# A delta-rule attention and feed-forward kernel: half of the triangular blocks inverted by GpSimd during the projection, key norms taken by token, key products stored unmasked, ScalarE copying only the blocks below the diagonal

## What is computed

```
q, k, v = silu(causal conv of 4 taps(x @ W.T));  beta = sigmoid(x @ Wb.T)
q, k = q/|q|, k/|k|                                  # norms by head and token
# per head, in chunks:  M = I + tril(beta*k @ k.T, -1);  T = M^-1
# u = T @ (beta*v);  w = T @ (beta*k)
# scan:  u_adj = u - w @ S;  o = q @ S + tril(q @ k.T) @ u_adj;  S += k.T @ u_adj
o = p0*fir3(v) + p1*fir15(v) + p2*fir63(v) + p3*o + p4*v     # p: softmax gates
x = layernorm(x + rmsnorm(o) @ Wo.T)
x = layernorm(x + ffn(x))                                    # 256-1024-1024-1024-256
```

## Time and profile before

| | us |
|---|---|
| median of three runs (2434.59 to 2437.62) | 2437.59 |
| the profiled execution | 2435.2 |
| its span in the trace | 2433.3 |
| projection, weights and FIR, recurrence: start | 0, 360.45, 612.28 |
| feed-forward: start | 1098.46 |
| TensorE, VectorE, ScalarE, GpSimd busy | 2157.0, 1235.5, 895.2, 593.4 |

### The profile page before, as it was taken

How to read it: one execution, slowest core, us unless ns; L and a number is a source line. 1 busy time by engine, 2 the same in 40 slices (tenths; PEclk the granted TensorE clock), 3 DMA queues, 4 the chain that set the end, 5 groups by cost and what they waited for, 6 DMA issues and landing times.

```text
span 2433.3 us, 40589 instructions
## 1 busy us (share of the span) xinstructions
PE 2157.0 (89%) x15412; PEld 1855.9 (76%) x15412; DVE 1235.5 (51%) x1872; ACT 895.2 (37%) x1425; POOL 593.4 (24%) x416
## 2 busy tenths in 40 slices
PE   7887865655699999967999999999999999999998
PEld 6776754555588888855888888888888888888887
DVE  5776758896477777762323332333333333323332
ACT  4554530002233334313434443444344334433442
POOL 2555555896344444430000000000000000000000
PEclk9999987887799999987999999999999999999999
DMA  3558759787989989925000000000000000000000
GB/s 131 194 197 204 194 200 211 198 207 236 241 229 249 250 235 241 254 79 219 1 18 17 0 17 17 17 0 17 17 17 0 17 17 17 0 17 17 18 1 18
DMA packets 346603, 257.53 MB, mean 106 GB/s; under 512 B 281394, under 2 KB 315698, under 8 KB 336434
## 3 DMA queue, kind: packets, MB, share of 16 engines
q1 hardware_dynamic: 333682, 232.65, 35.1%
q10 hardware_dynamic: 12864, 24.12, 2.8%
HBM read 156.85 MB, written 99.88 MB: 106 GB/s over the span
## 4 chain that ended last, share of the span: by engine, by line
PE 52%; issue 1%; DVE 1%; ACT 0%; DMA 0%; SPq 0%; POOL 0%; DVEq 0%; ACTq 0%; POOLq 0%
PE B L1611 46%; PE O L1639 5%; PE T L1567 1%; DVE yb L1738 0%; ACT gate L1677 0%; DMA wr<-wr_s 0%; SPq L1500 0%; DVE stats L1769 0%; ACT L1677 0%; DVE z L1764 0%; DVE z L1760 0%; DVE z L1783 0%; POOL rstd L1819 0%; SPq L1514 0%; DVEq L1733 0%
## 5 line engine op out<-in xcount | busy, mean ns | idle before, releaser
L1611 PE MATMUL B<-act1l,wr 128*128 128x512 f32 x1024 | 398.4, 389 | 0.0
L1611 PE MATMUL B<-act1h,wr 128*128 128x512 f32 x1024 | 398.3, 389 | 0.0
L1611 PE MATMUL B<-act0h,wr 128*128 128x512 f32 x1024 | 398.3, 389 | 0.0
L1611 PE MATMUL B<-act0l,wr 128*128 128x512 f32 x1024 | 398.3, 389 | 0.0
L1691 ACT ACTIVATE yb<-B,scol 128x512 f32<-128x512 f32 x256 | 176.2, 688 | 581.0 <-PE B L1611 581.0
L1726 DVE TENSOR_TENSOR act0l<-yb,act0h 128x512 fp32r<-128x512 f32 x256 | 176.1, 688 | 377.9 <-ACT act0h L1694 375.7
L1816 POOL TENSOR_TENSOR rstd<-mv,ln_eps 128x4 f32<-128x4 f32 x16 | 3.2, 199 | 1309.2 <-DVE mv L1777 1309.2
L379 DVE SCALAR_TENSOR_TENSOR acc<-proj,taps,acc 128x512 f32<-128x512 f32 x288 | 214.4, 750 | 92.3 <-ACT acc L334 83.7
L1726 DVE TENSOR_TENSOR act1l<-yb,act1h 128x512 fp32r<-128x512 f32 x128 | 88.6, 692 | 295.5 <-ACT act1h L1694 295.5
L224 PE MATMUL proj<-xt,w_qkv 128*128 128x262 f32 x768 | 195.0, 400 | 35.9 <-DMA xt<-in_xt 19.4
L1611 PEld LDWEIGHTS B<-act1h,wr 128*128 128x128 f32 x1024 | 192.2, 188 | 39.9
(11 more groups left out here) (164 smaller groups left out, 3477.6 us busy)
## 6 DMA issues: line engine op xcount, KB each, us to landing
qk_s<-yT SPq DMA_DIRECT2D x16, 1024.0 KB, 5.8
kk_s<-kfull SPq DMA_DIRECT2D x16, 1024.0 KB, 3.9
qk<-qk_s SPq DMA_DIRECT2D x16, 1024.0 KB, 6.7
lt<-kk_s SPq DMA_DIRECT2D x15, 1024.0 KB, 5.3
wraw<-in_ffn_w ACTq DMA_DIRECT2D x16, 704.0 KB, 6.4
wr_s<-wround ACTq DMA_DIRECT2D x16, 704.0 KB, 9.5
toe<-in_firp SPq DMA_DIRECT2D x64, 160.0 KB, 3.6
xt<-in_xt SPq DMA_DIRECT2D x16, 524.0 KB, 4.0
```

What stands on the lines that cost most here:

```text
L1611: last = nc.tensor.matmul(B[slot % 4][:, :], w, part, start=(k == 0 and i == 0), stop=(k == kts - 1 and i == len(parts) - 1))
```

## The change

- **Projection.** GpSimd no longer picks diagonals or masks. It squares the keys by token (`sqk`, from `ktok`), and VectorE reduces that, 128x1024 in place of 128x512, into `kk`. `kfull` is stored once, unmasked, as soon as it is copied; `a_s` is gone; after each step four DMAs bring its blocks from `kk_s` into `tri`.
- After step 8 VectorE computes the block scales of the first 8 steps (`first_scales`, after one Exp on ScalarE); TensorE turns them and ScalarE copies them out in step 10. GpSimd then runs the substitution of those blocks (4 of 8 slots), in steps 10 to 15 and after the last, columns 1 to 24.
- **Weights and FIR.** GpSimd zeroes the other half's upper parts, runs columns 25 to 30 and the row scaling of its half, then enters the loop. VectorE does the other half, both operations of a column in each of the first 30 groups. `toe` is laid out in full on the host and comes as one DMA of 768 KB for each 8 channels. `d_s` and `t_s` are stored by halves after the loop's SyncE iterations 2, 4, 18 and 20.
- **Recurrence.** VectorE zeroes `nmat` once; ScalarE copies N in three pieces of a bank (only what lies below the diagonal blocks); and the copies of round A stand ahead of the wait for `mixed`.

```diff
+EARLY_COLS = {10: (1, 5), 11: (5, 9), 12: (9, 12), 13: (12, 15), 14: (15, 18), 15: (18, 21), 16: (21, 25)}
+EARLY_END = 25
-def blocks_in(queue, io, keep, part):
+def blocks_in(queue, io, keep, t):
+    first = t * NS % P
     for q in range(NQ):
+        queue.dma_start(keep["tri"][first:first + NS, q * NSUB + t // EARLY_STEPS, :, :],
+                        io["kk_s"][q * CH:q * CH + CH, t * NS:t * NS + NS, q * CH:q * CH + CH].rearrange("i n j -> n i j")
+                        ).then_inc(keep["tri_in"][t // EARLY_STEPS], 16)
+class Substitution:
+    def outer_product(self, j):
+        row = self.tri[:, :, j, 0:j]
+        row = bass.AP(tensor=row.tensor, offset=row.offset, ap=[row.ap[0], row.ap[1], [0, CH - 1 - j], row.ap[2]])
+        return self.engine.tensor_tensor(self.products(j), bcast(self.tri[:, :, j + 1:CH, j], j), row, ALU.mult)
+    def update(self, j):
+        below = self.tri[:, :, j + 1:CH, 0:j]
+        return self.engine.tensor_tensor(below, below, self.products(j), ALU.add)
...
@@ project: SyncE
                     sp.wait_ge(kk_out, 4 * n)
-                    for q in range(NQ):
-                        sp.dma_start(io["a_s"][rows, bass.ds(t * NS, NS), :], kfull[p][rows, :, rows]).then_inc(diag_stored[p], 16)
+                    sp.dma_start(io["kk_s"][:, t * NS:t * NS + NS, :], kfull[p][:, :, :]).then_inc(kk_stored[p], 16)
...
-                    sp.wait_ge(kk_masked, n)
-                    sp.dma_start(io["kk_s"][:, bass.ds(t * NS, NS), :], kfull[p][:, :, :]).then_inc(kk_stored[p], 16)
+                    sp.wait_ge(kk_stored[p], 16 * (t // 2 + 2))
+                    blocks_in(sp, io, keep, t)
@@ project: VectorE, values_out
-                    dve.wait_ge(diag_picked, t * NQ + NQ)
...
-                    nc.vector.tensor_reduce(kk[...], picked[p][:, :, :], AX.X, ALU.add).then_inc(kk_summed, 1)
+                    dve.wait_ge(sqk_done, t + 3)
+                    nc.vector.tensor_reduce(kk[...], sqk[:, :, :].rearrange("p b (h d) -> p (b h) d", d=DK), AX.X, ALU.add).then_inc(kk_summed, 1)
@@ project: GpSimd
+                for t in range(STEPS + 1):
+                    if t < STEPS:
+                        squares(t, t % 2)
+                    if t:
+                        key_squares(t - 1, 1 - t % 2)
...
+                    if t in EARLY_COLS:
...
+                        early_columns(nc, pool, sub, keep, first, end)
@@ weights_fir: VectorE
                 for n in range(NGRP):
                     weigh(n)
-                    j = n // 2 + 1
-                    if j <= COLS:
-                        link(outer_product(j) if n % 2 == 0 else update(j))
+                    if n < COLS:
+                        link(sub.outer_product(n + 1))
+                        link(sub.update(n + 1))
@@ weights_fir: GpSimd
-                for i in range(2):
-                    nc.gpsimd.memset(toe[i][:, :, :, :], 0.0).then_inc(toe_zero, 1)
+                late = Substitution(nc.gpsimd, keep, 1, None)
+                pool.wait_ge(tri_in[1], 16 * NQ * EARLY_STEPS)
+                late.zero_above().then_inc(above_zero, 1)
+                sub = Substitution(nc.gpsimd, keep, 0, keep["outer0"])
+                early_columns(nc, pool, sub, keep, EARLY_END, CH - 1)
+                pool.wait_ge(keep["sub_link"], 2 * (CH - 1))
+                sub.scaled_rows().then_inc(inv_done[0], 1)
@@ delta: ScalarE
+        BELOW = ((slice(CH, 2 * CH), slice(0, CH)), (slice(2 * CH, P), slice(0, 2 * CH)), (slice(3 * CH, P), slice(2 * CH, 3 * CH)))
+                        if kind == "N":
+                            for rows, cols in BELOW:
+                                last = nc.scalar.activation(nmat[rows, c, cols], bank[rows, :, cols], ACT.Copy)
...
+                    if pre:
+                        copy_rounds("A", seq, round0)
                     act.wait_ge(mixed, t + 1)
                     nc.scalar.activation(osq[:, :, :, :], o[:, :, :, :], ACT.Square).then_inc(sq_done, 1)
                     if pre:
-                        copy_rounds("A", seq, round0)
                         copy_rounds("B", seq, round0)
```

More of the change, by code:

```diff
@@ new lines, with __init__, scaled_columns, products @@
+class Substitution:
+    def __init__(self, engine, keep, half, outer):
+        self.engine, self.slots = engine, slice(half, SLOTS, NSUB)
+        self.tri, self.outer = keep["tri"][:, self.slots, :, :], outer
+        self.gamT, self.neg_gamT = keep["gamT"][:, self.slots, :], keep["neg_gamT"][:, self.slots, :]
+    def scaled_columns(self):
+        for r in range(0, CH, 8):
+            g = self.neg_gamT[:, :, 0:r + 8]
+            g = bass.AP(tensor=g.tensor, offset=g.offset, ap=[g.ap[0], g.ap[1], [0, 8], g.ap[2]])
+            last = self.engine.tensor_tensor(self.tri[:, :, r:r + 8, 0:r + 8], self.tri[:, :, r:r + 8, 0:r + 8], g, ALU.mult)
+        return last
+    def products(self, j):
+        return self.outer[:, 0:SLOTS // NSUB * (CH - 1 - j) * j].rearrange("p (s i c) -> p s i c", s=SLOTS // NSUB, c=j)
+    def outer_product(self, j):
[5 more added lines that the diff above has]
+        return self.engine.tensor_tensor(below, below, self.products(j), ALU.add)
+    def scaled_rows(self):
+        return self.engine.tensor_tensor(self.tri, self.tri, bcast(self.gamT, CH), ALU.mult)
+    def zero_above(self):
+        for i in range(CH - 1):
+            last = self.engine.memset(self.tri[:, :, i, i + 1:CH], 0.0)
+        return last
+    def ones_on_diagonal(self):
+        return self.engine.memset(self.tri.rearrange("p s i j -> p s (i j)")[:, :, 0:CH * CH:CH + 1], 1.0)
@@ L190, in _ @@
                 sp.dma_start(io["v_s"][:, WIN:P, 0, :, :].rearrange("h p b d -> p h (b d)"), zero[:, :, :]).then_inc(zero_stored, 16)
[L191 to L195, removed]
-                    done = end
-                    if end < STEPS:
-                        for p in range(2):
-                            sp.wait_ge(diag_stored[p], end // 2 * (16 * NQ))
-                        blocks_in(sp, io, keep, part)
-                for p in range(2):
-                    store(STEPS - 2 + p, p, False)
+                for t in range(STEPS):
+                    store(t, t % 2, t + 2 < STEPS)
                 for p in range(2):
@@ L293, in _ @@
                 step(0, 0, 0, False)
-                with pe.Fori(0, STEPS // 2 - 1) as i:
+                with pe.Fori(0, EARLY_STEPS // 2) as i:
+                    step(i * 2 + 1, 1, i, True)
+                    step(i * 2 + 2, 0, i + 1, True)
+                for t in range(EARLY_STEPS + 1, EARLY_STEPS + 3):
+                    step(t, t % 2, t // 2, True)
+                with pe.Fori(EARLY_STEPS // 2 + 1, STEPS // 2 - 1) as i:
                     step(i * 2 + 1, 1, i, True)
@@ L469, in weights_fir, with early_columns @@
+def early_columns(nc, pool, sub, keep, first, end):
+    for j in range(first, end):
+        pool.wait_ge(keep["sub_link"], 2 * j)
+        sub.outer_product(j).then_inc(keep["sub_link"], 1)
+        pool.wait_ge(keep["sub_link"], 2 * j + 1)
+        sub.update(j).then_inc(keep["sub_link"], 1)
 def weights_fir(nc, sems, io, keep):
```

262 lines of the change are left out of this document (128 added, 134 removed).

## The result

The change made the kernel slower: 2450.6 us in the median (2448.2 to 2454.2, 4 runs) against 2436.1 us (2431.0 to 2437.6, 4 runs), a ratio of 1.0064, with a 95% interval of 1.0044 to 1.0085. The forecast was 2408 us, with 2385 to 2432 as its range. The profiled execution has a span of 2452.4 us, 19.1 more than the 2433.3 of before; it is the slowest of its four, and by the medians the kernel lost 14.5 us.

What follows compares the result with a forecast made beforehand. It saw the second stage's loop as where the change pays (VectorE busy 177, GpSimd 179 of 201 us). Terms -0.5 - 5 - 26 - 8 + 10.5 = -29 us took 2435.2 to 2406 profiled, 2408 median; range 2385 to 2432.

Steps and rivals of the forecast that it cites:

- the rival on the other side: Projection: GpSimd too slow for short rows, VectorE waiting for key squares from 3 ns an element; 2463 at 4; 7%.
- The early scales: Projection: table loads, a short Exp and linked VectorE operations for the first blocks' scales, costing +3.5 us once.
- If nothing collides, 385; if the scaling waits for all of GpSimd's row scaling, 395. I take 390: Second stage's head: time of the first product, depending on VectorE and GpSimd excluding each other; taken as -5 us.
- 63 + 10: Loop, last 33 groups: TensorE binds at 1.92 us a group, 63 us, plus 10 us of waiting.
- The load is uneven, so I keep half of the wait, 10 us: Loop: of VectorE's 19.5 us waiting for TensorE's late groups, 10 us remain, with DMA at 76% of the loop.
- my own sign of being wrong beyond 10 us: Loop: TensorE waiting for windows beyond 10 us in all would show the forecast wrong.
- My rival of a DMA-bound loop: Loop: second half waits for windows and `toe` with inverse stores between; 190 in place of 175 us, 2423; 15%.
- The 1.5 and 1.55 us a group for TensorE at full clock: Loop, last 33 groups: 1.5 in the 160 us bound; 1.55 without DMA waits in a rival giving 2386, 14%.
- the term of 0.7 us for the late square: Recurrence: the square waits for the fourth copy of A and starts 0.7 us later, fifteen steps, +10.5 us.
- stay under TensorE's 0.95 us a bank, and nothing waits for the last: nothing: Recurrence: nine small copies of N, about 0.75 us a bank, keep pace with TensorE and cost nothing.
- The rival that the copies of A help: Recurrence: TensorE's saved wait gives -1 us a step, 25 us less, 2383; 12%.

Runs made afterwards that it cites:

- the run with early windows: Changed kernel with A copied behind the square, a third table buffer, and the next head's windows fetched two parts at a time behind four tables: 2403.0 us.
- the run with the order alone: Kernel before, with only ScalarE's copies of A moved ahead of the square: 2457.7 us, 1.0096 of before.
- the half-ahead run: Changed kernel with two of A's four banks copied ahead of the square and two behind it: 2429.7 us, 0.9974 of before.
- the square first: Changed kernel with ScalarE again copying A behind the square of the outputs: 2427.2 us, 0.9975 of before.
- the pieces: Kernel before, with only the copies of N in three pieces a bank added: 2446.3 us, 1.0048 of before.
- the masked load: Changed kernel with A copied behind the square, only the blocks that count loaded into a cleared buffer, and N copied whole: 2417.3 us, 0.9928 of before.
- the late square: Kernel before, with a copy of 128x384 into a spare buffer right ahead of the square, A still behind it: 2442.1 us, 1.0028 of before.

## Why the prediction was wrong

- **Projection** (-0.5 forecast, +0.9 measured): right in the main. The step of 28.6 us is gone. GpSimd's tail ends the stage as described (its last update ends at 361.04, where 359.5 was forecast). It kept pace in steps 10 to 15 with 3.7 to 5.4 us idle before the next step's squares (3 forecast), and instructions of 960 elements took 1.9 to 2.2 us, so the rival on the other side was wrong in its mechanism. (Its average of 5280 elements a step is 4853 by the columns of the change, which puts its threshold at 3.3 ns and not 3.) TensorE's side was not right: its last value copy came 2.1 us later (353.75 against 351.64) where 0.5 earlier was forecast. The early scales cost more than their 3.5 us, two steps of 23.9 and 23.3 us instead of 20.3, and GpSimd's tail hides it.
- **Up to the first product** (-5, measured -2.2): the term "If nothing collides, 385; if the scaling waits for all of GpSimd's row scaling, 395. I take 390" took the middle where the rows offered one end. (390 against 395.15 also counts the projection's 0.5 a second time.) The table of taps on VectorE, 1280 elements with two SBUF inputs, took 2.31 us alone in the kernel before and 9.10 here, beside GpSimd's 8.23 us: it ended 2.2 us after GpSimd did. It was this instruction that waited, and not the column scaling. The Trainium skill (SBUF — State Buffer, "Who interferes with whom") has the two exclude each other for the whole instruction; taken strictly, that was 395. The trace agrees with the rule: the first product came at 393.87.
- **Loop** (-26, measured -4.1): the first 30 groups took 95.3 us (96.8 forecast), the group with the row scaling 5.2 (5.3). The 95.3 are in part luck: 4 us of them are late transfers, and in the run with early windows these groups took 91.4, so their price was 5 us too high. The rest was forecast at 63 + 10 and took 98. The step that failed is "The load is uneven, so I keep half of the wait, 10 us". I had counted only what reached VectorE, 19.5 us, where TensorE waited 40 us for transfers, and its waits for windows, my own sign of being wrong beyond 10 us, stood at 25.2 before the change and at 22.2 after it. And I had priced the transfers by their bytes, 76% of the loop. That share came out as said (0.76), and it is not what binds. What binds is another sum: a table lands 5.6 us after its issue (the median), behind windows and 2 MB stores in SyncE's order; with two buffers it may take 3.84, the time of the two groups before it. With three buffers and early windows these 33 groups took 76.4 us, near the 73 of the forecast. My rival of a DMA-bound loop named the waits that came, for windows and `toe` with the inverse stores between them; its 190 was too small, and its cause, the bytes, was not the one. The 1.5 and 1.55 us a group for TensorE at full clock did not follow from the rows either: 1.92 at a clock of 0.85 makes 1.63.
- **End of the stage** (-8, measured -8.3): right.
- **Recurrence** (+10.5, measured +32.8): the term of 0.7 us for the late square is right to 0.01 (28.02 against 27.32 in the run with the order alone). Two others were wrong. The copies of N were to "stay under TensorE's 0.95 us a bank, and nothing waits for the last: nothing". They are twelve and not nine, and a bank takes 0.96 us and not 0.75; that still keeps pace, but `Q` waits for the last one, 0.66 us a step, 9.9 in all. And no term asked what becomes of TensorE's idle time: 1.4 us before B and 0.35 before N became one stretch of 2.1 to 2.5, and N ran at a lower granted clock (0.67 in the mean of the round measured) in 9 of 13 steps, 1.45 us each, 13 us. 10.5 + 9.9 + 13 = 33.4. The rival that the copies of A help was wrong; the half-ahead run shows that round B can end 0.9 us earlier and the step does not.
- **Sum.** 22 us from the recurrence, 22 from the loop, 3 from the head and 1 from the projection turn -29 into +19. That is the profiled execution; the medians moved by 14.5, and in which stage the other executions lost less isn't shown.

## What to carry to other kernels

Work moved ahead "into a wait" needs two checks: who stands behind it in the same engine's queue, and whether the waits that it shifts on TensorE close up into one long enough to cost clock. A copy that keeps pace with its producer can still be late with its last piece, so look at who waits for the last one. And a prefetch is sized by its time from issue to landing, with what is queued ahead of it, against the time its buffers cover: 50.7 MB in 197 us looked like room to spare, and one buffer and one change of order were worth 24 us (2427.2 to 2403.0).

## What the runs showed of the hardware beside that

- The granted clock does not follow the length of the idle stretch alone. With the order alone N took 5.44 us behind 2.22 us of idle time at 845.12 and 3.81 behind the same 2.22 at 1018.12, and both behind 2.51. It was long in 9 rounds of 13 in the changed kernel, in 6 of 13 in the kernel before with the order alone. In the runs with the square first, the pieces, the masked load, half ahead and the late square, at most 1.53 us were idle before N in these rounds, and it was never long. Granted 1.00 is 2.4 GHz and 0.50 is 1.2 GHz; the 0.67 of a whole round is a mean over both.
- With packets of 6 KB in place of short ones (10,774 against 75,459 in the loop) the rate was 257 GB/s instead of 203, at a share of 0.76 against 0.78: a quarter more bytes in the same DMA time.
- GpSimd's row scaling, which reads SBUF, costs VectorE's instructions with two SBUF inputs their overlap, whether in one piece of 8.2 us or four of 1.9: 6.4 us gained ahead of the loop, 5.5 lost in its first five groups.
